# One four-batch MetaFormer kernel: square roots by Exp and Ln in the front, gate on raw rows, last scan chunk in halves

## The reference

```python
x = x + L0_conv(_ln_c(x))    # LayerNorm; four Mamba scans of 64 channels; skip; LayerNorm; projection
t = t + L0_ffn(_ln_t(t))     # input and weight rounded to fp8, one 256x256 product, bias
x = x + L1_conv(_ln_c(x))    # GroupNorm over 32 groups, attention between channels, projection
t = t + L1_ffn(_ln_t(t))     # 8 experts, the best 2 of each token by gate logits, GELU between two products
def step(h, inp):            # inside L0_conv: 16 states, 1024 tokens
    dA = jnp.exp(dt_t[:, :, None] * A)
    h = dA * h + (dt_t * x_t)[:, :, None] * B_t[:, None, :]
    y = jnp.einsum('bds,bs->bd', h, C_t)
def _ln_t(v, eps=1e-05):
    m = jnp.mean(v, axis=-1, keepdims=True)
    s = jnp.var(v, axis=-1, keepdims=True)
    return (v - m) / jnp.sqrt(s + eps)
```

## Time and profile before

| | |
|---|---|
| median of 3 runs | 1981.06 us (1978.47 to 1984.16) |
| the profiled execution | 1983.14 us |
| its span in the trace | 1981.2 us |
| busy in the span | PE 1528.7, DVE 1346.4, POOL 1166.9, ACT 767.4 us |
| front for the first batch | 0 to 102.9 us |
| four stages of scans | 206.90, 207.60, 207.20, 207.00 us |
| three stages between | 121.90, 124.30, 124.70 us |
| the last one, without a next batch | 100.1 us |
| routing; experts | 51.50; 527.1 us |

### The profile page before, as it was taken

The page is one execution under the profiler, slowest core; times in us unless marked ns, Lnnn a source line. Parts: engine busy times, 40 slices in busy tenths (PEclk is TensorE's granted clock), DMA queues, the critical chain, the costliest instruction groups (busy, mean ns, idle before and its releaser), DMA issues. The chain is left out here.

```text
span 1981.2 us, 20702 instructions
## 1 busy us (share of the span) xinstructions
PE 1528.7 (77%) x5773; PEld 941.8 (48%) x5806; DVE 1346.4 (68%) x1441; ACT 767.4 (39%) x1201; POOL 1166.9 (59%) x605
## 2 busy tenths in 40 slices
PE   5467678867677886777786677767369999999997
PEld 2122224542222453222444222235258888888887
DVE  2899998579999768999867899983642222222222
ACT  6535334654442664444277353322112222222222
POOL 0699892359987038989513998930045554545543
PEclk9689999979999997999998899988579999999999
DMA  3075560146554015646202655653102222222222
GB/s 117 27 270 198 189 204 23 41 166 215 193 180 139 23 61 202 211 163 214 84 22 83 243 202 181 207 219 137 66 24 41 33 40 35 38 37 37 37 33 27
DMA packets 80697, 230.71 MB, mean 116 GB/s; under 512 B 12844, under 2 KB 31605, under 8 KB 77270
## 3 DMA queue, kind: packets, MB, share of 16 engines
q1 hardware_dynamic: 64694, 210.93, 30.6%
q0 software_dynamic: 15904, 18.66, 5.9%
HBM read 208.15 MB, written 19.82 MB: 115 GB/s over the span
## 5 line engine op out<-in xcount | busy, mean ns | idle before, releaser
L390 PE MATMUL psum<-HC_sb,ident_sb 128*128 128x512 f32 x1024 | 493.7, 606 | 65.1 <-DVE HC_sb L1362 57.4
L390 PE MATMUL psum<-experts_sb 64*128 64x512 f32 (+5 forms) x930 | 307.7, 562 | 240.6 <-DVE HC_sb L1362 149.3
L952 ACT ACTIVATE psum<-experts_sb 128x1024 f32<-128x1024 f32 x256 | 285.5, 1117 | 506.8 <-DVE experts_sb L1352 393.8
L1352 DVE TENSOR_TENSOR_SCAN experts_sb<-psum,DBX_sb 128x1024 f32<-128x1024 f32 x172 | 389.7, 2275 | 31.7 <-POOL DBX_sb L1042 30.7
L390 PEld LDWEIGHTS psum<-HC_sb,ident_sb 128*128 128x128 f32 x1024 | 190.0, 192 | 282.0 <-issue 131.8
L390 PEld LDWEIGHTS psum<-experts_sb 64*128 64x128 f32 (+5 forms) x962 | 97.9, 153 | 473.9 <-DVE HC_sb L1362 240.7
L1886 DVE TENSOR_TENSOR YS_sb<-psum_moe,b_sb 128x256 f32<-128x256 f32 x71 | 30.1, 424 | 353.5 <-PE psum_moe L1641 349.9
L1734 ACT ACTIVATE hgt_sb<-psum_moe,b_sb 128x256 f32<-128x256 f32 (+1 forms) x312 | 116.5, 456 | 381.2 <-PE psum_moe L1641 381.2
L1641 PE MATMUL psum_moe<-XGT_sb,w1s_sb 128*128 128x256 f32 (+1 forms) x1248 | 253.6, 362 | 0.0
L1641 PE MATMUL psum_moe<-experts_sb,hgt_sb 128*128 x1136 | 251.7, 379 | 0.7 <-DVE YS_sb L1886 0.7
L1618 POOL DMA_INDIRECT out<-YS_sb,scat_sb x71 | 131.7, 1855 | 203.9 <-DVE YS_sb L1890 188.7
(11 more groups left out here) (264 smaller groups left out, 1742.7 us busy)
## 6 DMA issues: line engine op xcount, KB each, us to landing
DA_sb<-bc_rows SPq DMA_DIRECT2D x128, 512.0 KB, 4.6
experts_sb<-bc_rows SPq DMA_DIRECT2D x64, 512.0 KB, 3.7
SQ_sb<-bc_rows SPq DMA_DIRECT2D x64, 512.0 KB, 4.2
X_XT_sb<-bc_rows SPq DMA_DIRECT2D x64, 512.0 KB, 5.5
experts_sb<-w1T SPq DMA_DIRECT2D x8, 1024.0 KB, 19.3
experts_sb<-w2T SPq DMA_DIRECT2D x8, 1024.0 KB, 21.3
X_sb<-x_tok SPq DMA_DIRECT2D x5, 1024.0 KB, 7.1
experts_sb<-x_tok SPq DMA_DIRECT2D x4, 1024.0 KB, 4.8
```

The lines of the kernel that those rows point to most:

```text
L390: return nc.tensor.matmul(o, lhsT, rhs, start=start, stop=stop, **k)
L952: nc.scalar.activation(decays[i % 2], DT[:, c, :], ACT.Exp, scale=a_neg[:, s:s + 1]).then_inc(da_ready, 1)
L1352: v.tensor_tensor_scan(STATE[i % STATE_SLOTS], decays[i % 2], DRIVE[i % STATE_SLOTS], 0.0, ALU.mult, ALU.add).then_inc(h_ready, 1)
```

## The change

All of it is in `build_front`; `build_moe` is as it was.

- The product of `first_small` goes from DVE to GpSimd (`first_shift`), after drive 33.
- `POOL_READS` moves one step ahead: GpSimd reads out the steps 2, 6, 10 and 14 of a chunk, so that the chunk's last state is read by DVE.
- After the last chunk, gate, projection and skip go in two halves of 512 tokens, and the turn of y starts after the first.
- The FFN bias becomes one more matmul per 128 tokens (three bf16 parts times ones), `add_ffn_bias` goes away; `x2` adds to X1.
- The group root and the last LayerNorm's root become Ln and Exp(-0.5 x) on ACT with one Newton step on DVE (four small operations for the group, three for the tokens: `last_rstd`).
- The gate product takes the raw x3, turned (`tm_turn` waits for the adds alone), with gate weights that have their mean taken out; `route` multiplies the logits by the reciprocal root. The normalised rows for the experts are written by DVE (`last_norm`, eight 128x256), no longer by ACT.
- `steps_of_dt(b, 3)` moves from the end of GpSimd's front to behind drive 2 of the scans. `log1p(b, 1)` stands whole ahead of the softmax, `log1p(b, 2)` whole behind x3, then `last_rstd`, `last_norm`, `route`, then `log1p(b, 3)`. SP's loads for step 2 and on also wait for the first two steps of `log1p(b, 3)`, whose memory they take. PE's z products go behind the gate product.

The diff, cut to its core (the rest renumbers waits, moves PE's and ACT's calls to match, and adds to the preparation of weights):

```diff
-POOL_READS = (3, 7, 11, 15)
+POOL_READS = (2, 6, 10, 14)
...
-            sp.wait_ge(dt_done, NC)
+            sp.wait_ge(sp_step, NC * SP_STEPS)
...
                 sp.wait_ge(gate_done, b)
+                sp.wait_ge(sp_step, b * (NC * SP_STEPS) + ((NC - 1) * SP_STEPS + 2))
...
             def y_turn(p):
                 for k in range(4):
+                    if k == 0:
+                        pe.wait_ge(ym_half, p + 1)
+                    if k == 2:
+                        pe.wait_ge(ym_done, (p + 1) * NC)
...
+                        at = psum[:, k, (n % 2) * C:(n % 2 + 1) * C]
+                        mm(at, ones_b[:, :], FB_PARTS[:, :], True, False)
...
-                pe.wait_ge(tm_done, p * NB + (4 * h + 4))
-                if h:
-                    pe.wait_ge(x3_done, p * 4 + 4)
+                pe.wait_ge(x3_done, p * 4 + (2 + 2 * h))
...
                 hc_turn(p, 0)
+                if go_on:
+                    dt_linear(b, 2)
                 group_var(p)
-                if go_on:
-                    bc_linear(b)
                 hc_turn(p, 1)
                 scores(p)
                 if go_on:
-                    dt_linear(b, 2)
                     dt_linear(b, 3)
+                    bc_linear(b)
                 attend(p)
-                if go_on:
-                    z_pair(b, 0)
                 out_linear(p)
-                if go_on:
-                    z_pair(b, 1)
                 tm_turn(p, 0)
                 tm_turn(p, 1)
                 gate(p)
+                if go_on:
+                    z_pair(b, 0)
...
+                        if i == NI - 1 and h == 0:
+                            m.then_inc(ysum_half, 1)
...
-                    pe.wait_ge(yf_ready, b * NC + c + 1)
                     p0 = DM * (c % 2)
                     for h in range(NH):
+                        if c == NC - 1 and h == 0:
+                            pe.wait_ge(yf_half, b + 1)
+                        else:
...
+            def token_rsqrt(p):
+                for h in range(NH):
+                    m = slice(4 * h, 4 * h + 4)
+                    act.wait_ge(mv_done[3], p * 2 + h + 1)
+                    nc.scalar.activation(token_std[:, 3, m], token_mv[:, 3, m, 1], ACT.Ln, bias=eps5[:, :]).then_inc(log_done, 1)
+                    act.wait_ge(log_done, p * 3 + (h + 2))
+                    nc.scalar.activation(token_rs[:, 3, m], token_std[:, 3, m], ACT.Exp, scale=-0.5).then_inc(std_done[3], 1)
...
-                nc.scalar.activation(g_std, psum[:, 0, 0:2], ACT.Sqrt, bias=eps5[:, :]).then_inc(g_std_ready, 1)
+                nc.scalar.activation(g_log, psum[:, 0, 0:2], ACT.Ln, bias=eps5[:, :]).then_inc(log_done, 1)
+                act.wait_ge(log_done, p * 3 + 1)
+                nc.scalar.activation(g_rs, g_log, ACT.Exp, scale=-0.5).then_inc(g_std_ready, 1)
...
-                steps_of_dt(b, 3)
...
+            def between(b):
+                pool.wait_ge(g_step, b * 5)
+                steps_of_dt(b, 0)
+                steps_of_dt(b, 1)
+                split_bc(b)
+                steps_of_dt(b, 2)
+
+            def first_shift(b):
+                pool.wait_ge(f_small, b * 2 + 1)
+                nc.gpsimd.tensor_tensor(f_nb[:, :], f_neg[:, :], f_rs[:, :], ALU.mult).then_inc(f_small, 1)
...
                     drive(i)
+                    if i == STATE_SLOTS - 1:
+                        steps_of_dt(b, NC - 1)
+                    if i == FIRST_AT + 2 * NB + NB // 2 + 1:
+                        first_shift(b + 1)
...
-                dve.wait_ge(f_small, b * 2 + 1)
-                v.tensor_tensor(f_nb[:, :], f_neg[:, :], f_rs[:, :], ALU.mult).then_inc(f_small, 1)
...
-                    dve.wait_ge(x1f_done, p * 2 + k // 2 + 1)
                     v.scalar_tensor_tensor(X2[:, m, :], psum[:, k, :].rearrange("p (n c) -> p n c", n=2), scal[:, 5:6],
-                                           X2[:, m, :], ALU.mult, ALU.add).then_inc(x2_done, 1)
+                                           X1[:, m, :], ALU.mult, ALU.add).then_inc(x2_done, 1)
...
+
                 dve.wait_ge(g_std_ready, p + 1)
-                v.reciprocal(g_rs, g_std).then_inc(g_step, 1)
-                dve.wait_ge(g_step, p * 6 + 3)
+                v.tensor_tensor(g_fix, psum[:, 0, 0:2], g_rs, ALU.mult).then_inc(rsqrt_step, 1)
+                dve.wait_ge(rsqrt_step, p * 7 + 1)
+                v.scalar_tensor_tensor(g_fix, g_rs, 1e-5, g_fix, ALU.mult, ALU.add).then_inc(rsqrt_step, 1)
+                dve.wait_ge(rsqrt_step, p * 7 + 2)
+                v.scalar_tensor_tensor(g_fix, g_fix, -0.5, g_rs, ALU.mult, ALU.mult).then_inc(rsqrt_step, 1)
+                dve.wait_ge(rsqrt_step, p * 7 + 3)
+                v.scalar_tensor_tensor(g_rs, g_fix, 1.5, g_rs, ALU.add, ALU.mult).then_inc(rsqrt_step, 1)
+                dve.wait_ge(rsqrt_step, p * 7 + 4)
...
                 add(0)
+                add(1)
                 stat_of(0)
-                add(1)
                 stat_of(1)
                 means(3, p, 0)
                 add(2)
+                add(3)
                 stat_of(2)
-                rstd(3, p, 0)
-                add(3)
                 stat_of(3)
                 means(3, p, 1)
-                rstd(3, p, 1)
...
+            def last_rstd(p):
+
+                rs, var = token_rs[:, 3, :], token_mv[:, 3, :, 1]
+                dve.wait_ge(std_done[3], p * 2 + 2)
+                v.scalar_tensor_tensor(token_fix[:, :], var, 1e-5, rs, ALU.add, ALU.mult).then_inc(rsqrt_step, 1)
+                dve.wait_ge(rsqrt_step, p * 7 + 5)
+                v.scalar_tensor_tensor(token_fix[:, :], token_fix[:, :], -0.5, rs, ALU.mult, ALU.mult).then_inc(rsqrt_step, 1)
+                dve.wait_ge(rsqrt_step, p * 7 + 6)
+                v.scalar_tensor_tensor(rs, token_fix[:, :], 1.5, rs, ALU.add, ALU.mult).then_inc(rsqrt_step, 1)
+                dve.wait_ge(rsqrt_step, p * 7 + 7)
+
+            def last_norm(p):
+                for n in range(NB):
+                    v.tensor_scalar(TM[:, n, :], X2[:, n, :], token_mv[:, 3, n, 0:1], token_rs[:, 3, n:n + 1], ALU.subtract,
+                                    ALU.mult).then_inc(tm_done, 1)
 
             def route(p):
                 dve.wait_ge(gate_ready, p + 1)
-                v.tensor_copy(logits[:, bass.ds(p * NB, NB), :],
-                              psum[:, 2, 0:NB * E].rearrange("p (n e) -> p n e", n=NB)).then_inc(gate_done, 1)
+                v.tensor_tensor(logits[:, bass.ds(p * NB, NB), :], psum[:, 2, 0:NB * E].rearrange("p (n e) -> p n e", n=NB),
+                                token_rs[:, 3, :].unsqueeze(2).broadcast_to((P, NB, E)), ALU.mult).then_inc(gate_done, 1)
...
-                    log1p(b, 1, (0, 1, 2))
+                    log1p(b, 1)
                 softmax(p)
-                if go_on:
-                    log1p(b, 1, (3,))
                 weigh(p)
-                if go_on:
-                    log1p(b, 1, (4,))
                 out_weight(p)
-                if go_on:
-                    log1p(b, 2, (0,))
                 x3(p)
                 if go_on:
-                    log1p(b, 2, (1, 2, 3, 4))
+                    log1p(b, 2)
+                last_rstd(p)
+                last_norm(p)
+                route(p)
+                if go_on:
                     log1p(b, 3)
-                route(p)
...
+                def last_chunk():
+                    c, p0 = NC - 1, DM * ((NC - 1) % 2)
+                    for h in range(NH):
+                        at = slice(h * HL, (h + 1) * HL)
+                        if h == 0:
+                            dve.wait_ge(ysum_half, b + 1)
+                            dve.wait_ge(op_ready, b * NC + c)
+                        else:
+                            dve.wait_ge(ysum_done, b * NI + NI)
+                        v.tensor_tensor(YF[:, at], psum[:, 6 + h, :], SZ[:, c, at],
+                                        ALU.mult).then_inc(yf_ready if h else yf_half, 1)
+                    for h in range(NH):
+                        at = slice(h * HL, (h + 1) * HL)
+                        if h == 0:
+                            dve.wait_ge(op_half, b + 1)
+                        else:
+                            dve.wait_ge(op_ready, b * NC + c + 1)
+                        v.scalar_tensor_tensor(YM[p0:p0 + DM, c // 2, at], xn[p0:p0 + DM, c // 2, at], scal[p0:p0 + DM, 0:1],
+                                               psum[p0:p0 + DM, 2 + h, :], ALU.mult,
+                                               ALU.add).then_inc(ym_done if h else ym_half, 1)
...
-                gate(NC - 1)
-                skip(NC - 1)
+                last_chunk()
```

More of the change, by code:

```diff
@@ L137, in build_front @@
         token_nb = sb("token_nb", [P, LNS, NB])
[L138 to L140 removed]
+        small = sb("small", [P, 24])
+        g_sq, g_log, g_rs, g_sc, g_raw, g_var, g_fix = (small[:, 2 * i:2 * i + 2] for i in range(7))
+        s_max, s_neg, s_sum, s_rec = (small[:, 14 + 2 * i:16 + 2 * i] for i in range(4))
```

(3 more changed lines are left out.)

153 lines of the change are left out of this document (72 added, 81 removed).

## The result

| | before | after |
|---|---|---|
| median | 1979.76 us (1978.11 to 1984.16, 4 runs) | 1951.97 us (1950.39 to 1953.36, 4 runs) |
| profiled execution, span | 1983.14, 1981.2 | 1953.36, 1951.6 |

A forecast was written before the change was run, and what follows sets the result against it. DVE was taken to bound the scans (206.20 of 206.90 us busy), a chain of waits the stages between. Terms -22.4, -6.4, +6.6, -0.5 and +2.7 sum to -20.0, from the median 1981.06 to 1961.0 us; range 1946 to 1974.

The forecast's parts named there:

- Step 1: Scans: moving the 128x8 product to GpSimd frees DVE of a stall, 5.6 us per batch, -22.4 us in all.
- rival D: Scans: the shift wins nothing because the 5.8 us wait comes back elsewhere; 1983.5 us, chance 0.07.
- Step 2: Tail of a batch: last read-out on DVE and halved gate and skip save 1.6 us, four times, -6.4 us.
- Step 3: The three stages between, up to the seventh scan: +2.2 us each, +6.6 us in all.
- (f): Head of the scans: GpSimd is behind with late loads and the chunk-3 pair; seventh scan 2.2 us late.
- (d): Stage between, after log1p(2): 9.6 us of DVE steps and 9.4 us of GpSimd products exclude each other.
- (a): Stage between, up to the attention: many small changes, taken at +0.6 us, bounded by -2.36 and +2.0.
- (b): Stage between, x3: output product not behind z, no wait for ACT's root, two fewer reciprocals; 3.4 us saved.
- Step 4: Last front: the store of the normalised rows ends it in place of the logits, -0.5 us.
- step 5: First front: drive 0 starts earlier but drive 6 has the chunk-3 pair ahead of it, +2.7 us.
- Rival B: Stages between: only half of the 9.4 us of GpSimd products excludes DVE, 14.1 us less; 1947 us, chance 0.13.
- Rival C: Scans: GpSimd sets the pace, a stage taking 209.7 us; slower, 1994.6 us, chance 0.05.

The follow-up runs named there:

- no_shift: The changed kernel with the 128x8 product put back on DVE behind its reciprocal: 1975.08 us, against 1951.45 for the changed kernel on the same chip.
- shift_only: The kernel before, with only the 128x8 product moved from DVE to GpSimd behind drive 33: 1973.25 us, ratio 0.9955.
- reads_only: The kernel before, with only POOL_READS moved one step ahead and the 128x8 product still on DVE: 1989.38 us, ratio 1.0035.
- residual_late: The changed kernel with three of GpSimd's four residual additions moved from scan steps 23, 27, 31 to 49, 50, 51: 1945.46 us, ratio 0.9810.
- dt1_behind: The changed kernel with GpSimd's chunk-1 pair moved behind the split of B and C rows: 1940.81 us, ratio 0.9795.
- pair_spread: The changed kernel with GpSimd's chunk-3 products moved from behind drive 2 to behind drives 20 and 36, one each: 1947.28 us, ratio 0.9825.
- loads_first: The changed kernel with pair_spread's and residual_late's moves, B's row for scan step 3 issued first and the 1 MB load behind step 6: 1937.54 us.
- drives_early: loads_first with GpSimd's chunk-1 pair between the softmax's last multiplication and the split, and batches 1 to 3's chunk-2 pair behind drives 0 and 1: 1915.72 us.

## Why the prediction was right, and where its sizes were off

The direction, the range and most of the mechanisms held; the sum was 9.6 us short of the difference of the spans, with errors of both signs in it: step 1 gained 5.8 us less than forecast, the other terms 15.4 more, so that the total came this near is partly luck. And by one sign that the prediction gave for being wrong, a stage between over 5 us shorter, it was: from the last scan's end to the next first scan the three take 116.3, 118.8 and 117.8 us, where they took 121.9, 124.3 and 124.7.

*Step 1* was mis-sized: 5.6 us a stage forecast, 4.1 measured. The price of the stall (5.8) and of the product on GpSimd (0.2) were right, and the scan does not wait for GpSimd: the rows above show it at 2260 to 2293 ns as before. So rival D fell. With it fell, for this place, the Trainium skill's warning that such a move "might not help" (page "Perfetto Trace Analysis", section "Optimizing Scalar/DVE Operations"): undoing the move costs 23.6 us here (no_shift). What the sum lacked is the read-outs' price among the scans. Their new place leaves drives 25, 29 and 33 behind a residual addition and a read-out, and 1.26 us a stage went to the scans that wait for them, ahead of the steps 34 to 38 that the text named as the place to look. That GpSimd lost the lead that the stall gave it, as the prediction feared, is not the cause: shift_only has no such wait, reads_only has those at 25 and 29 with the stall still in place, and residual_late gives all three back. (Only the one at 33, 0.46 us, is absent where the stall stands.) Missed too is that the term hangs on step 2: with the last read-out still on GpSimd the gate gives 2 to 4 us of the 5.8 back (shift_only), and the prediction counted the read-outs' move for the tail alone.

*Step 2* was right in kind and short in size: 2.0 a batch against 1.6. Of it the read-out makes 1.2 to 1.3 (reads_only), the halves the rest, by difference; they were not run alone.

*Step 3* was forecast +2.2 a stage and measured -0.5 to -1.5. (e) and (f) came as described: the first scan directly behind the last softplus step, the 7th late. (d), the mutual exclusion, was right in kind and 1.3 us too high: from the end of log1p(2) to that of log1p(3) the change takes 17.7 us, 19.0 were counted; GpSimd's share fell on the norms, while log1p(3) went free because GpSimd waited for its row.

The step that failed is (a), the stretch up to the attention: forecast at +0.6, it takes 0.9, 2.4 and 3.3 us less in the three stages (from the first y statistics to DVE's first step on the attention's product). (b) then brings 2.3 to 3.5 of its 3.4. Together log1p(2) goes on 4.4, 4.7 and 6.1 us earlier (the point that the prediction puts at 408.6), where 2.8 were forecast. Some of this could have been read before: beside GpSimd's bias addition, a 128x4 multiplication in the FFN's normalisation stood 1.16 us in each batch, and it is not in the changed kernel. In the first stage DVE comes to the FFN 1.2 us earlier; no run tests this part alone.

```profile
331.51 1.16 DVE L1141 TENSOR_SCALAR token_rs_sb<-token_rs_sb,scal_sb 128x4 f32<-128x4 f32 x1
```

And (a) looked for GpSimd's price in the softplus alone. Two steps of log1p(1) do wait, 3.25 us each, where two took 1.94 and 3.03 before; but the softmax's small multiplications pay for the chunk-1 pair besides, and sparing them is worth 4 us a stage, with the faster matmuls behind them (dt1_behind).

*Step 4* had the mechanism (the store ends the front), with 2 us too little; *step 5* was 2.3 us too high: scan 6 comes at 120.98, 0.4 later than before, because drive 0 starts at 96.45, where 98.8 was counted.

Rival B's point, a shorter stage between, was nearer than the forecast's for step 3, but not by its mechanism, since the 9.4 us did mostly exclude DVE. Rival C did not decide: DVE waits for GpSimd at 5 of 64 scans. It came nearest in reads_only, where a stage takes 208.6 to 210.8 us, but there too DVE waits for a drive at three or four scans, and the stall is still in the stage.

Not settled: which small changes brought the rest of what 3 (a) gained, and whether the time from the norms' store to its landing could be hidden in the last front.

## What to carry to other kernels

A stall on the busiest engine can be paying for something: before its removal is priced, walk through what the neighbours did in that time (here the last read-out of a chunk), since the same edit brought 9 us alone and 24 us in company. When two waits end at about the same time, removing one can show nothing (pair_spread, batches 1 to 3); remove both before judging either. And place the products of GpSimd where DVE reads PSUM: the moves of this kind make 22 us (loads_first to drives_early), and all moves in its list and of two transfers, with the same arithmetic, 36 us, more than the whole change.
